# A transformer layer with attention and mixture of experts on one core: second-half gathers that add into x while they are transferred

## The chip, the cores and the metric

The kernel runs on one core of a Trainium2 chip. The metric is the time of one execution on the device, in microseconds (us), lower is better. Three runs of the kernel before gave 713.87, 715.39 and 716.93 us; their median is 715.39 us. A difference of about 0.5% is what a measurement of this kernel can tell from no change.

## The reference

The input is `x` of 32 batches x 256 tokens x 128 features. Each token is normalised, and three things are added up: the input, an attention over the 256 tokens of its batch, and the output of the two best of eight experts for that token.

```python
xn = _layernorm(x)
x = x + attention(xn, Wq, Wk, Wv, Wo, We) + ffn(xn, gate_w, w1, b1, w2, b2)

# attention: 16 heads of 8 features, one more term common to all heads
influence = einsum('bqe,bke->bqk', xn @ We.T, xn @ We.T)
scores = einsum('bhqd,bhkd->bhqk', Q, K) * SCALE + 0.1 * influence[:, None]
out = softmax(scores) @ V ... @ Wo.T

# ffn: the two most probable of 8 experts, weighted by their probabilities
h = gelu(x @ w1[expert] + b1[expert]);  y = h @ w2[expert] + b2[expert]
out = sum over the two choices of y * topk_probs
```

## The kernel before

The 8192 tokens lie as 64 tiles of 128 tokens in `x` (128 partitions, 64 tiles, 128 features, float32), where input and partial results are summed. A batch `b` has the tiles `2b` and `2b+1`. The work has four stages.

**Opening.** Load, normalise, transpose, choose experts for every token. `pos[j]` gets, for each token and each of its two choices `j`, the row of the slot that it occupies in the experts' sorted list.

**Attention for batches 0 to 15 (first half).** One step per batch. A step is a software pipeline over `k`: it projects batch `k+3` (letter `p` in the code), loads the stacked queries and keys of batch `k+2` (`l`), takes plain products and their row maxima for batch `k+1` (`m`), shifted products, exponentials and values for batch `k` (`x`), normalises batch `k-1` (`o`), and adds the attention of batch `k-2` into `x` (`c`, DVE line 970). `attention_steps` writes the first and last steps out and lets a loop on each engine run over the rest, two steps to a turn. A step is 8 units `u`; in each, TensorE makes two shifted products (line 1133), and each raises the semaphore `s_ex` by one, so `s_ex` reaches `16b + n + 1` after the shifted product `n` of batch `b`. ACT takes the exponential of each (line 708) and DVE the maxima of the plain products (line 956). SyncE's queue loads the stack for TensorE (lines 326, 330 and 334, then the maxima at 364 and the projections at 341 to 345), let go by `s_ex`, `s_mt`, `s_hq` and `s_lq`. GpSimd scatters the normalised rows to their slots in DRAM meanwhile (line 565).

**Experts.** 71 tiles of 256 slots go through the experts; the weighted results are stored in `slots_y` in DRAM, one row of 128 floats (512 bytes) per slot.

**Attention for batches 16 to 31 (second half).** The same steps. In addition GpSimd fetches the experts' results. In its loop `n` runs from 0 to 15 (`HALF` is 16) and serves four tiles: the two of batch `n` and the two of batch `16 + n`. Eight indirect DMAs (line 609), `m` from 0 to 7, gather 128 rows each: `j = m // 4` is the choice, `i = m % 4` the tile. They write into the buffer `ye2[n % 2]`, which overlays the tensor `rows`, so the profile calls it `rows`. Each waits until TensorE has reached a place in the step for batch `15 + n` (`LEAD` is 8, so the eight are spread over eight units). `add_choices` (line 594) then adds the second choice's four tiles to the first's, and `add_experts` (line 600) adds the sum into `x`. These two stand in GpSimd's queue behind the gathers `m == 3` and `m == 5` of the next `n`. `s_sum` tells DVE, two steps later, that the experts' part of batch `16 + n` is in `x`; DVE adds the attention's part, raises `s_acc`, and SyncE's queue stores the two batches `n` and `16 + n` (lines 445 and 447).

Nothing but waits and the queues' own order sets the sequence on an engine: each engine runs its own list, written out by the code.

Of the kernel before, what the change touches and what calls it, by code (L numbers as in the profile page):

```python
# [19 lines left out]
F32 = mybir.dt.float32  # L20
# [3 lines left out]
ALU = mybir.AluOpType  # L24
# [4 lines left out]
D = 128  # L29
# [29 lines left out]
LEAD = 8  # L59
HALF = B // 2  # L60
# [72 lines left out]
def build(nc, X, Wsmall, Wo, W12, B1, B2, out):  # L133
    with ExitStack() as ctx:
        def sb(name, shape, dt):
            return ctx.enter_context(nc.sbuf_tensor(name, shape, dt))

        def sem(name):
            return ctx.enter_context(nc.semaphore(name))
# [3 lines left out]
        slots_y = nc.dram_tensor("slots_y", [ET * SLOT, D], F32, kind="Internal").ap()  # L143
# [5 lines left out]
        x = sb("x", [P, NT, D], F32)  # L149
# [32 lines left out]
        pos = [sb(f"pos{i}", [P, NT], U32) for i in range(2)]  # L182
# [32 lines left out]
        free = rows[:, :, :].rearrange("p t d -> p (t d)")  # L215
        at = [0]

        def carve(n, dt):
            v = free[:, at[0]:at[0] + n * (2 if dt == F32 else 1)]
            at[0] += n * (2 if dt == F32 else 1)  # L220
            return v.bitcast(F32) if dt == F32 else v
# [4 lines left out]
        hp = [carve(2 * FC * SLOT, F16).rearrange("p (a f s) -> p a f s", a=2, f=FC) for _ in range(2)]  # L226
        ye = [carve(2 * D, F32).rearrange("p (s d) -> p s d", s=2) for _ in range(4)]
        b2 = carve(NE * D, F32)
        ye2 = [free[:, 16 * D * i:16 * D * (i + 1)].bitcast(F32).rearrange("p (m d) -> p m d", m=8) for i in range(2)]
        assert at[0] <= NT * RW  # L230


# [32 lines left out]
        s_ex, s_xp, s_pv, s_pe = (sem(n) for n in ("s_ex", "s_xp", "s_pv", "s_pe"))  # L265
# [1 line left out]
        s_xr = [sem(f"s_xr{i}") for i in range(4)]  # L267
        s_sp = [sem(f"s_sp{i}") for i in range(3)]
        s_fu, s_fg, s_fh, s_fa, s_fl, s_fd, s_fy = (sem(n) for n in ("s_fu", "s_fg", "s_fh", "s_fa", "s_fl", "s_fd", "s_fy"))
        s_yp, s_both, s_sum = sem("s_yp"), sem("s_both"), sem("s_sum")  # L270
        s_ys = [sem(f"s_ys{i}") for i in range(4)]
        s_yg = [[sem(f"s_yg{r}_{m}") for m in range(8)] for r in range(2)]
        s_cw = [sem(f"s_cw{i}") for i in range(4)]
# [27 lines left out]
        def _(sp):  # L301
            sp.dma_start(ws_stage, Wsmall).then_inc(s_ws, 16)
            for q, sm in enumerate(s_x):
                n = slice(q * NT // 4, (q + 1) * NT // 4)
# [133 lines left out]
            def attend_store(s, f, k):  # L438
                attend(s, f, k, False)
                if f["c"]:  # L440
                    b = s.at(-2)[0]
                    sp.wait_ge(s_acc, b + 1 if isinstance(b, int) else sp.to_reg(b + 1))
                    for n in (b - HALF, b):
                        if isinstance(n, int):
                            sp.dma_start(out_v[n], x[:, 2 * n:2 * n + 2, :]).then_inc(s_out, 16)
                        else:
                            sp.dma_start(out_v[bass.ds(n, 1)].rearrange("n p s d -> (n p) s d"), x[:, bass.ds(2 * n, 2), :]).then_inc(s_out, 16)
# [6 lines left out]
        def _(pool):  # L454
# [56 lines left out]
            for g in range(NG):  # L511
# [5 lines left out]
                for j in range(2):  # L517
                    t = 4 * g + j
# [37 lines left out]
            for j in range(2):  # L556
                for t in range(NT):
                    n = NT * j + t
# [26 lines left out]
            for i, sm in enumerate(s_ys):  # L585
                pool.wait_ge(sm, 16 * ((ET - i + 3) // 4))

            halves = x[:, :, :].rearrange("p (h t) d -> p h t d", h=2)

            def add_choices(n):  # L590

                for m in range(8):
                    pool.wait_ge(s_yg[n % 2][m], 16 * (n // 2) + 16)
                pool.tensor_tensor(ye2[n % 2][:, 0:4, :], ye2[n % 2][:, 0:4, :], ye2[n % 2][:, 4:8, :], ALU.add).then_inc(s_both, 1)

            def add_experts(n):

                pool.wait_ge(s_both, n + 1)
                pair = halves[:, :, 2 * n:2 * n + 2, :]
                pool.tensor_tensor(pair, pair, ye2[n % 2][:, 0:4, :].rearrange("p (h t) d -> p h t d", h=2), ALU.add).then_inc(s_sum, 1)  # L600

            for n in range(HALF):
                for m in range(8):
                    j, i = m // 4, m % 4
                    t = 2 * n + i if i < 2 else 2 * (n + HALF) + i - 2
                    pool.wait_ge(s_ex, 16 * (HALF + n) + 2 * (m - LEAD) + 2)
                    if n >= 2:
                        pool.wait_ge(s_sum, n - 1)
                    pool.indirect_dma_start(ye2[n % 2][:, m, :], None, slots_y, bass.IndirectOffsetOnAxis(pos[j][:, t:t + 1], 0)).then_inc(s_yg[n % 2][m], 16)  # L609
                    if m == 3 and n:  # L610
                        add_choices(n - 1)
                    if m == 5 and n:
                        add_experts(n - 1)
            add_choices(HALF - 1)
            add_experts(HALF - 1)


        @block.scalar
# [144 lines left out]
        def _(dve):  # L763
# [167 lines left out]
            def attend(s, f, k, first_half=True):  # L931
                b, par, half = s.at(0)
                b1_, par1, half1 = s.at(1)
                for u in range(8):
                    if first_half and (k, u) in ((HALF, 2), (HALF, 6), (HALF + 1, 2)):
                        experts.load({(HALF, 2): 3, (HALF, 6): 12}.get((k, u), EW))
                    if first_half and k == HALF and u == 0:
                        dve.wait_ge(s_whi, NCH)
                        for h in range(2):
                            cols = slice((2 * NCH - 2 + h) * WCH // 2, (2 * NCH - 1 + h) * WCH // 2)  # L940
                            dve.scalar_tensor_tensor(out=w12[:, 1, cols], in0=w_stage[:, h * WCH // 2:(h + 1) * WCH // 2], scalar=FS, in1=w12[:, 0, cols], op0=ALU.mult, op1=ALU.subtract).then_inc(s_wlo, 1)
                    if k == -1 and u == 6:
                        prefix()
                    if k == 0 and u == 0:
                        counted()
                    if k == 0 and u == 2:
                        probs()
                    if k == 0 and u == 4:
                        tile_experts()
                    if k == 0 and u == 7:  # L950
                        tile_words()
                    if f["m"]:
                        g, qt = u // 2, u % 2
                        a = g // 2
                        dve.wait_ge(s_mx, 8 * b1_ + u + 1)
                        dve.tensor_reduce(mx[:, a, 8 * qt:8 * qt + 8].rearrange("q (i e w) -> q i e w", i=2, e=2)[:, :, g % 2], MX[u % 2][:, :].rearrange("q (i w k) -> q i w k", i=2, w=2), AX.X, ALU.max).then_inc(s_red, 1)  # L956
                        if u in (3, 7):
                            dve.wait_ge(s_red, 8 * b1_ + 4 * a + 4)
                            if k is None or b1_ >= 2:
                                dve.wait_ge(s_mr[par1][a], 32 * half1)  # L960
                            for i in range(4):
                                ins = dve.transpose(mT[:, par1, a, 32 * i:32 * i + 32], mx[32 * i:32 * i + 32, a, :])  # L962
                            ins.then_inc(s_mt, 1)
                    if u == 0 and f["c"]:
                        bc = s.at(-2)[0]
                        if not first_half:
                            dve.wait_ge(s_sum, bc - HALF + 1)
                        dve.wait_ge(s_wo, bc + 1)
                        xs_ = x[:, 2 * bc:2 * bc + 2, :] if isinstance(bc, int) else x[:, bass.ds(2 * bc, 2), :]
                        dve.tensor_tensor(xs_, xs_, MISC[:, S:2 * S].rearrange("p (q d) -> p q d", q=2), ALU.add).then_inc(s_acc, 1)  # L970
                    if u == 2 and f["p"]:
                        b3_ = s.at(3)[0]
                        dve.wait_ge(s_hq, b3_ + 1)
                        dve.scalar_tensor_tensor(out=lo_qk[:, :, :].rearrange("p a t -> p (a t)"), in0=MISC[:, :], scalar=1 / WS,
                                                 in1=hi_qk[:, :, :].rearrange("p a t -> p (a t)"), op0=ALU.mult, op1=ALU.subtract).then_inc(s_lq, 1)
                    if u == 5 and f["o"]:
                        bo = s.at(-1)[0]
                        dve.wait_ge(s_ot, bo + 1)
                        v = MISC[:, :].rearrange("q (h r) -> q h r", r=16)
                        dve.reciprocal(rden[:, :], v[:, :, DK]).then_inc(s_rd, 1)  # L980
                        dve.wait_ge(s_rd, bo + 1 + c_rd)
                        if k is None or bo >= 1:
                            dve.wait_ge(s_oT, bo)
                        dve.tensor_tensor(o_n[:, :, :, :].rearrange("p q h d -> p (q h) d"), v[:, :, 0:DK], rden[:, :].unsqueeze(2).to_broadcast([P, 2 * H, DK]), ALU.mult).then_inc(s_on, 1)
# [305 lines left out]
```

## Time and profile before

| | |
|---|---|
| runs of the kernel before | 713.87, 715.39, 716.93 us |
| span of the profiled execution | 791.5 us |
| PE, DVE, ACT, POOL busy in it | 671.2, 619.4, 538.9, 467.2 us |
| attention, first half, 116 to 340 us | PE busy 195.61 of 224 us |
| experts, 348 to 536 us | PE busy 187.03 of 188 us |
| entry of the second half, 545 to 570 us | PE busy 12.24 of 25 us |
| second half in its loop, 600 to 745 us | PE busy 131.98 of 145 us |

The profiled execution is one execution and 76.1 us longer than the median of the runs without a profile; what lies around its span is part of that difference and isn't shown apart. Durations below are those of the profiled execution. In the rows, L609 is line 609 of the kernel before, `<-` stands between what is written and what is read, and the brackets at a row's end give how long the engine stood idle before it and which event ended that.

### The profile page before, as it was taken

The page shows a single profiled execution, that of the slowest core. Times are in us where ns is not written, and L with a number is a line of the kernel's source. Part 1 is how long each engine was busy: PE and PEld are TensorE (multiplying, and loading weights), DVE is VectorE, ACT ScalarE, POOL GpSimd, SP SyncE. Part 2 cuts the span into 40 slices and gives each one's busy share as a digit, 9 for nine tenths or more (in the row PEclk, how much of TensorE's full clock was granted, in tenths as well). Part 3 has the DMA queues.
Part 4 walks back from the last instruction along what each step waited for, and adds up shares of the span by engine and source line. Part 5 has one row for each costly group of instructions (what it writes and reads, how often), then busy time and mean ns, then how long its engine had stood idle before and what let it go on. Part 6 is the DMA issues. An engine that isn't in the chain of part 4 may idle for free.

```text
span 791.5 us, 24553 instructions
## 1 busy us (share of the span) xinstructions
PE 671.2 (85%) x7800; PEld 433.1 (55%) x7800; DVE 619.4 (78%) x1106; ACT 538.9 (68%) x1123; POOL 467.2 (59%) x542
## 2 busy tenths in 40 slices
PE   0477888989889896969999999996689989988886
PEld 0463344444444443559999999993244444444444
DVE  8989878878778785948888888885587888887871
ACT  2581566776667685858888888884466766766765
POOL 8650656666566555306555565656676676676671
PEclk9997899999999998999999999999699999999998
DMA  9779545665455653664555454443376666566632
GB/s 262 253 212 299 138 125 146 154 175 158 117 159 148 176 155 100 174 111 90 101 105 102 96 109 102 103 89 100 77 153 161 159 165 166 152 161 161 159 92 61
DMA packets 162947, 113.32 MB, mean 143 GB/s; under 512 B 72624, under 2 KB 150448, under 8 KB 162864
## 3 DMA queue, kind: packets, MB, share of 16 engines
q1 hardware_dynamic: 153632, 90.63, 46.2%
q0 software_dynamic: 8192, 16.86, 8.6%
q10 hardware_dynamic: 1040, 4.76, 1.6%
q8 instruction: 48, 0.79, 0.4%
q14 instruction: 35, 0.29, 0.1%
HBM read 55.42 MB, written 47.19 MB: 130 GB/s over the span
## 4 chain that ended last, share of the span: by engine, by line
PE 71%; DVE 7%; issue 7%; SPq 5%; ACT 4%; another core or an unknown queue 3%; DMA 1%; ACTq 0%; DVEq 0%
PE bank L1133 20%; PE bank L1111 13%; PE bank L1251 12%; PE mx L1240 12%; PE mx L1145 7%; ACT A L708 4%; DVE mx L956 2%; PE bank L1193 2%; PE bank L1031 2%; PE bank L1162 2%; DVE A L791 2%; PE bank L1155 1%; SPq L319 1%; SPq L318 1%
## 5 line engine op out<-in xcount | busy, mean ns | idle before, releaser
L708 ACT ACTIVATE A<-bank 128x512 f32<-128x512 f32 x502 | 279.1, 602 | 109.9 <-PE bank L1133 94.1
L956 DVE TENSOR_REDUCE mx<-mx 128x4 f16<-128x1024 f32 x256 | 303.7, 1208 | 56.3 <-PE mx L1145 26.8
L1133 PE MATMUL bank<-stack 113*128 113x256 f16 x1004 | 185.2, 283 | 51.2 <-issue 24.9
L565 POOL DMA_INDIRECT slots_x<-rows,pos x128 | 123.5, 965 | 91.3 <-PE bank L1133 68.0
L579 POOL TENSOR_SCALAR rows<-rows,slot_p 128x128 f32<-128x128 f32 x142 | 112.1, 798 | 103.4 <-DVE rows L1007 103.4
L609 POOL DMA_INDIRECT rows<-slots_y,pos x128 | 121.5, 950 | 73.4 <-PE bank L1133 54.6
L1133 PEld LDWEIGHTS bank<-stack 113*128 113x128 f16 x1004 | 66.9, 99 | 164.9 <-issue 85.7
L1111 PE MATMUL bank<-A,V 128*32 128x256 f32 x2048 | 142.2, 397 | 1.7 <-ACT A L708 1.6
L752 ACT ACTIVATE rows<-mx,b 128x256 f32<-128x256 f32 x284 | 111.8, 474 | 30.0 <-PE mx L1240 30.0
L1001 DVE TENSOR_TENSOR rows<-rows 128x512 f16<-128x512 f32 x142 | 101.2, 714 | 25.2 <-ACT rows L756 22.8
L1251 PE MATMUL bank<-w,rows 128*128 x1704 | 108.2, 220 | 4.4 <-DVE rows L1001 4.4
L1251 PEld LDWEIGHTS bank<-w,rows 128*128 128x128 f16 x1704 | 102.0, 98 | 6.7 <-issue 4.6
L1240 PE MATMUL mx<-rows,w 128*128 128x256 f16 x852 | 105.4, 274 | 0.0
L1145 PE MATMUL mx<-stack 64*128 64x256 f16 (+1 forms) x1024 | 84.4, 279 | 11.9 <-DVE mx L956 4.5
L1240 PEld LDWEIGHTS mx<-rows,w 128*128 x852 | 80.8, 98 | 8.7 <-issue 0.2
L1111 PEld LDWEIGHTS bank<-A,V 128*32 128x32 f32 x2048 | 54.4, 111 | 50.9 <-issue 23.2
L697 ACT ACTIVATE O<-bank 128x256 f32<-128x256 f32 x64 | 24.7, 386 | 60.0 <-PE bank L1111 34.2
L1145 PEld LDWEIGHTS mx<-stack 64*128 64x128 f16 (+1 forms) x1024 | 36.6, 96 | 52.1 <-issue 30.6
L962 DVE STREAM_TRANSPOSE mT<-mx 32x32 f16<-32x32 f16 x256 | 51.2, 200 | 6.8
L756 ACT ACTIVATE rows<-rows 128x512 f16<-128x512 f32 x71 | 44.8, 630 | 6.7
L970 DVE TENSOR_TENSOR x<-x,bank 128x256 f32 (+1 forms) x32 | 13.5, 421 | 38.1 <-PE bank L1193 25.8
L1052 PE MATMUL mx<-ident,rows 128*128 128x128 f16 x128 | 13.4, 268 | 34.1 <-DVE rows L828 32.5
(142 smaller groups left out, 616.8 us busy)
## 6 DMA issues: line engine op xcount, KB each, us to landing
stack<-ctx_rest SPq DMA_DIRECT2D x64, 256.0 KB
stack<-qk_dram SPq DMA_DIRECT2D x128, 96.0 KB
slots_y<-rows SPq DMA_DIRECT2D x71, 128.0 KB, 2.0
qk_dram<-hi_qk SPq DMA_DIRECT2D x64, 128.0 KB
stack<-ctx_high SPq DMA_DIRECT2D x128, 64.0 KB
slots_x<-A ACTq DMA_DIRECT2D x1, 4644.0 KB, 20.2
w_stage<-in_w SPq DMA_DIRECT2D x8, 512.0 KB
qk_dram<-lo_qk SPq DMA_DIRECT2D x64, 64.0 KB
```

The lines of the kernel that those rows point to most:

```text
L565: pool.indirect_dma_start(slots_x, bass.IndirectOffsetOnAxis(pos[j][:, t:t + 1], 0), rows[:, t, :].bitcast(F32), None).then_inc(s_scat, 16)
L579: ins = pool.tensor_scalar(ye[n % 4][:, h, :], ye[n % 4][:, h, :], slot_p[:, n // 4 % 3, n % 4, h:h + 1], None, ALU.mult)
L609: pool.indirect_dma_start(ye2[n % 2][:, m, :], None, slots_y, bass.IndirectOffsetOnAxis(pos[j][:, t:t + 1], 0)).then_inc(s_yg[n % 2][m], 16)
L708: act.activation(A[:, n % NA, :, :].rearrange("p h s -> p (h s)"), scores(k, n)[:, :], ACT.Exp, scale=SCALE).then_inc(s_xp, 1)
L752: act.activation(h32[r % 2][:, fc, :], bank[fc][:, 0:SLOT], ACT.Gelu_apprx_tanh, bias=b1[:, bass.ds(e + fc, 1)], scale=1 / FS).then_inc(s_ ...
L956: dve.tensor_reduce(mx[:, a, 8 * qt:8 * qt + 8].rearrange("q (i e w) -> q i e w", i=2, e=2)[:, :, g % 2], MX[u % 2][:, :].rearrange("q (i ...
L1001: dve.tensor_tensor(lo, h, hi, ALU.subtract).then_inc(s_fl, 1)
L1111: mm = pe.matmul(PV[32 * i:32 * i + 32, 0:S], head_values(pp, c, g, i), A[:, (4 * g + 2 * c + i // 2) % NA, i % 2, :], start=(e == 0 and c ...
L1133: mm = pe.matmul(scores(k, n)[:, i * S:(i + 1) * S], stack[0:SHIFT + 1, par, h, 1, c * P:(c + 1) * P], stack[0:SHIFT + 1, par, h, 0, :], s ...
L1145: mm = pe.matmul(MX[v % 2][:, (2 * i + p) * S:(2 * i + p + 1) * S], stack[r0:r1, par1, h, 0, v % 2 * P:(v % 2 + 1) * P], stack[r0:r1, par1 ...
L1240: mm = pe.matmul(bank[fc][:, 0:SLOT], w1[:, pa, bass.ds(e + fc * P, P)], xt[r][:, pb, :], start=(n == 0), stop=(n == 2))
L1251: mm = pe.matmul(bank[6 + par][:, h * D:(h + 1) * D], hp[par][:, pa, fc, h * P:(h + 1) * P], w2[:, pb, bass.ds(e_before + fc * P, P)], sta ...
```

## The change

The buffer `ye2` and its two semaphores go. The gather writes with an addition straight into the tile of `x` (`compute_op=ALU.add`): the transfer reads what stands in `x`, adds and writes back. So the two gathers of one tile must not overlap, and the gather of the second choice (`m` 4 to 7) waits for the landing of the first choice's gather of that tile, four gathers before. GpSimd's two additions per `n` go. Each gather's wait on `s_ex` is one lower. DVE, ahead of its addition at batch `16 + n`, waits for the gathers 6 and 7 in the place of `s_sum`, and SyncE's queue, ahead of the stores, for the gathers 4 and 5. All else is the same.

```diff
-        ye2 = [free[:, 16 * D * i:16 * D * (i + 1)].bitcast(F32).rearrange("p (m d) -> p m d", m=8) for i in range(2)]
...
                 if f["c"]:
                     b = s.at(-2)[0]
                     sp.wait_ge(s_acc, b + 1 if isinstance(b, int) else sp.to_reg(b + 1))
+                    for m in (4, 5):
+                        sp.wait_ge(s_yg[s.r][m], 16 * (s.half - 1 - HALF // 2) + 16)
...
-            halves = x[:, :, :].rearrange("p (h t) d -> p h t d", h=2)
-
-            def add_choices(n):
-
-                for m in range(8):
-                    pool.wait_ge(s_yg[n % 2][m], 16 * (n // 2) + 16)
-                pool.tensor_tensor(ye2[n % 2][:, 0:4, :], ye2[n % 2][:, 0:4, :], ye2[n % 2][:, 4:8, :], ALU.add).then_inc(s_both, 1)
-
-            def add_experts(n):
-
-                pool.wait_ge(s_both, n + 1)
-                pair = halves[:, :, 2 * n:2 * n + 2, :]
-                pool.tensor_tensor(pair, pair, ye2[n % 2][:, 0:4, :].rearrange("p (h t) d -> p h t d", h=2), ALU.add).then_inc(s_sum, 1)
-
             for n in range(HALF):
                 for m in range(8):
                     j, i = m // 4, m % 4
                     t = 2 * n + i if i < 2 else 2 * (n + HALF) + i - 2
-                    pool.wait_ge(s_ex, 16 * (HALF + n) + 2 * (m - LEAD) + 2)
-                    if n >= 2:
-                        pool.wait_ge(s_sum, n - 1)
-                    pool.indirect_dma_start(ye2[n % 2][:, m, :], None, slots_y, bass.IndirectOffsetOnAxis(pos[j][:, t:t + 1], 0)).then_inc(s_yg[n % 2][m], 16)
-                    if m == 3 and n:
-                        add_choices(n - 1)
-                    if m == 5 and n:
-                        add_experts(n - 1)
-            add_choices(HALF - 1)
-            add_experts(HALF - 1)
+                    pool.wait_ge(s_ex, 16 * (HALF + n) + 2 * (m - LEAD) + 1)
+                    if j == 1:
+                        pool.wait_ge(s_yg[n % 2][m - 4], 16 * (n // 2) + 16)
+                    pool.indirect_dma_start(x[:, t, :], None, slots_y, bass.IndirectOffsetOnAxis(pos[j][:, t:t + 1], 0), compute_op=ALU.add).then_inc(s_yg[n % 2][m], 16)
...
                         if not first_half:
-                            dve.wait_ge(s_sum, bc - HALF + 1)
+                            for m in (6, 7):
+                                dve.wait_ge(s_yg[s.r][m], 16 * (s.half - 1 - HALF // 2) + 16)
```

GpSimd's list at the start of the second half, before (`rows` is the buffer `ye2`):

```order
262 L609 DMA rows<-slots_y,pos 128x128 [waits s_ys3,s_ys2,s_ex,s_ys1,s_ys0]
263 L609 DMA rows<-slots_y,pos 128x128 [waits s_ex] x11
264 L594 TENSOR_TENSOR rows<-rows 128x512 [waits s_yg0_4,s_yg0_5,s_yg0_3,s_yg0_6,s_yg0_2,s_yg0_7,s_yg0_1,s_yg0_0]
265 L609 DMA rows<-slots_y,pos 128x128 [waits s_ex] x2
266 L600 TENSOR_TENSOR x<-x,rows 128x2x256 [waits s_both]
267 L609 DMA rows<-slots_y,pos 128x128 [waits s_ex] x2
268 L609 DMA rows<-slots_y,pos 128x128 [waits s_sum,s_ex] x4
```

The same place in the changed kernel:

```order
262 L596 DMA x<-slots_y,pos 128x128 [waits s_ys3,s_ys2,s_ex,s_ys1,s_ys0]
263 L596 DMA x<-slots_y,pos 128x128 [waits s_ex] x3
264 L596 DMA x<-slots_y,pos 128x128 [waits s_yg0_0,s_ex]
265 L596 DMA x<-slots_y,pos 128x128 [waits s_yg0_1,s_ex]
266 L596 DMA x<-slots_y,pos 128x128 [waits s_yg0_2,s_ex]
267 L596 DMA x<-slots_y,pos 128x128 [waits s_yg0_3,s_ex]
268 L596 DMA x<-slots_y,pos 128x128 [waits s_ex] x4
269 L596 DMA x<-slots_y,pos 128x128 [waits s_yg1_0,s_ex]
```

Nothing but gathers is left, and the second four of each eight wait for a landing.

DVE's addition of the attention's result, at the steps behind the loop, before:

```order
833 L970 TENSOR_TENSOR x<-x,bank 128x256 [waits s_wo,s_sum]
834 L956 TENSOR_REDUCE mx<-mx 128x2x2 [waits s_mx] x2
835 L974 SCALAR_TENSOR_TENSOR lo_qk<-bank,hi_qk 128x512 [waits s_hq]
836 L956 TENSOR_REDUCE mx<-mx 128x2x2 [waits s_mx]
```

and in the changed kernel:

```order
832 L952 TENSOR_TENSOR x<-x,bank 128x256 [waits s_wo,s_yg0_7,s_yg0_6]
833 L937 TENSOR_REDUCE mx<-mx 128x2x2 [waits s_mx] x2
834 L956 SCALAR_TENSOR_TENSOR lo_qk<-bank,hi_qk 128x512 [waits s_hq]
835 L937 TENSOR_REDUCE mx<-mx 128x2x2 [waits s_mx]
```

It stands in the same place and waits for one semaphore more. The lists of PE and ACT are the same in both kernels.

## Rows read from the trace of the kernel before

**Rows 1.** The page: the span, and busy time of each engine.

```profile
span 791.5 us, 24553 instructions
...
PE 671.2 (85%) x7800; PEld 433.1 (55%) x7800; DVE 619.4 (78%) x1106; ACT 538.9 (68%) x1123; POOL 467.2 (59%) x542
```

**Rows 2.** Busy time by stretch: us, then busy us of each engine.

```profile
core 0: us, PE busy (x) PEld busy (x) DVE busy (x) ACT busy (x) POOL busy (x), PEclk, DMA share, GB/s
...
545.00:570.00 25.00, 12.24 (x98) 4.65 (x92) 7.93 (x11) 8.12 (x16) 17.62 (x18) 0.66 0.42 99
...
600.00:745.00 145.00, 131.98 (x1483) 68.71 (x1476) 124.23 (x199) 101.38 (x207) 100.52 (x99) 1.00 0.66 163
```

**Rows 3.** Waits of PE, 600 to 745 us: engine line, waited for, us, times, longest.

```profile
PE bank L1133 <- ACT A L708: 9.4, 12, 1.1
PE mx L1145 <- issue: 0.8, 4, 0.2
PE mx L1145 <- DVE mx L956: 0.7, 1, 0.7
PE bank L1133 <- issue: 0.7, 2, 0.4
```

**Rows 4.** Timeline of DVE, line 970: start, duration, the instruction, idle before it.

```profile
581.39 0.42 DVE L970 TENSOR_TENSOR x<-x,bank 128x256 f32 x1 [0.92 <-PE bank L1193]
...
743.39 0.42 DVE L970 TENSOR_TENSOR x<-x,bank 128x256 f32<-128x256 f32 x1 [0.85 <-PE bank L1193]
...
788.32 0.42 DVE L970 TENSOR_TENSOR x<-x,bank 128x256 f32<-128x256 f32 x1 [2.30 <-PE bank L1193]
```

**Rows 5.** Groups of instructions of POOL: busy us, mean ns, idle before.

```profile
L609 POOL DMA_INDIRECT rows<-slots_y,pos x128 | 121.5, 950 | 73.4 <-PE bank L1133 54.6 <-issue 13.2 <-remote 3.2
...
L594 POOL TENSOR_TENSOR rows<-rows 128x512 f32<-128x512 f32 x16 | 20.5, 1284 | 3.7 <-DMA rows<-slots_y,pos 3.4
L600 POOL TENSOR_TENSOR x<-x,rows 128x512 f32<-128x512 f32 x16 | 20.4, 1277 | 0.4
```

**Rows 6.** Timeline of POOL: the first gather, part of one step, the last gather.

```profile
542.22 1.05 POOL L609 DMA_INDIRECT rows<-slots_y,pos  x1 [2.73 <-PE bank L1133]
...
618.98 0.95 POOL L609 DMA_INDIRECT rows<-slots_y,pos  x1 [0.16 <-issue]
620.24 0.95 POOL L609 DMA_INDIRECT rows<-slots_y,pos  x1 [0.30 <-issue]
621.21 1.27 POOL L600 TENSOR_TENSOR x<-x,rows 128x512 f32<-128x512 f32 x1
...
625.79 0.94 POOL L609 DMA_INDIRECT rows<-slots_y,pos  x1 [0.89 <-PE bank L1133]
...
772.47 0.95 POOL L609 DMA_INDIRECT rows<-slots_y,pos  x1 [0.30 <-issue]
776.80 1.27 POOL L594 TENSOR_TENSOR rows<-rows 128x512 f32<-128x512 f32 x1 [3.38 <-DMA rows<-slots_y,pos]
```

**Rows 7.** DMA queues and gathers, 600 to 745 us: share of 16 engines.

```profile
q1 hardware_dynamic: 22910, 18.30, 49.4%
q0 software_dynamic: 2538, 5.22, 16.8%
...
rows<-slots_y,pos POOLq DMA_INDIRECT x79
```

**Rows 8.** Timeline of one step: SP's transfer of maxima, the product that needs it.

```profile
618.89 1.36 SPq L364 DMA_DIRECT2D stack<-mT  x2
...
624.15 0.61 PE L1133 MATMUL bank<-stack 113*128 113x256 f16 x4
```

**Rows 9.** Timeline: long idle times of PE, ACT and DVE, first and second half.

```profile
305.87 0.59 PE L1133 MATMUL bank<-stack 113*128 113x256 f16 x2 [4.63 <-issue]
...
551.60 0.38 ACT L697 ACTIVATE O<-bank 128x256 f32<-128x256 f32 x1 [5.21 <-remote]
553.01 0.61 PE L1133 MATMUL bank<-stack 113*128 113x256 f16 x2 [5.63 <-issue]
558.01 1.22 DVE L956 TENSOR_REDUCE mx<-mx 128x4 f16<-128x1024 f32 x1 [11.38 <-remote]
561.51 1.10 PE L1133 MATMUL bank<-stack 113*128 113x256 f16 x4 [3.91 <-issue]
```

More of the change, by code:

```diff
@@ L269, in build @@
         s_fu, s_fg, s_fh, s_fa, s_fl, s_fd, s_fy = (sem(n) for n in ("s_fu", "s_fg", "s_fh", "s_fa", "s_fl", "s_fd", "s_fy"))
-        s_yp, s_both, s_sum = sem("s_yp"), sem("s_both"), sem("s_sum")
+        s_yp = sem("s_yp")
         s_ys = [sem(f"s_ys{i}") for i in range(4)]
```

## The prediction, made before the changed kernel ran

> **What bounds the kernel now.** I read the page's busy times first [rows 1], then the busy times by stretch [rows 2], because only the second half of the attention is touched. In its loop, from 600 to 745 us, PE is busy 131.98 of 145 us, which is 91%; DVE 124.23 us (86%), ACT 101.38 us and POOL 100.52 us (69%). The granted clock is 1.00 there. So the question is what PE waits for, and the view of its waits answers it [rows 3]: ACT for 9.4 us, and DVE and its own issue for 2.2 us. No wait on POOL and none on a DMA stands there. The step takes (743.39 - 581.39) / 11 = 14.73 us by twelve successive additions of DVE [rows 4].
>
> The same view of DVE's line 970 shows where an engine could meet POOL's work, for that instruction holds the wait on `s_sum`: in the 16 steps of the second half the idle before it is ended 14 times by PE's product with `wo`, as in [rows 4], and never by POOL. The reader is to see that POOL's additions have no customer that waits: they are made more than one step before DVE asks.
>
> **The two additions go.** POOL saves 16 x (1.284 + 1.277) = 41.0 us of busy time [rows 5], or 2.56 us per step. All of it lies beside PE's work: POOL holds 8 x 1.26 (one gather starts 1.26 us after the other when nothing holds it [rows 6]) + 2.56 + 0.3 = 12.9 us of the 14.73 us, and then stands until a shifted product lets it go, 0.89 us in the row shown [rows 6]. Worth on the path: 0. After the change POOL needs 10.1 us per step and waits longer for PE.
>
> At the end the last addition starts at 776.80 + 1.3 us and is over by about 779.4, while DVE's last two additions wait for PE, the last starting at 788.32 [rows 4, 6]. Nine microseconds of cover, so the end doesn't move by what leaves POOL: 0.
>
> **The release by the first product, not the second.** It lets a gather start up to one product sooner. The gathers are taken up by nobody for over a step, so 0 again. The clumps (three gathers 1.26 us apart between the additions) turn into single gathers, one per unit, some 14.73 / 8 = 1.84 us apart. That is kinder to the transfers of SP's queue, on which PE doesn't wait now: 0.
>
> **The wait for the first choice's landing.** Behind it in POOL's queue stand only further gathers. A landing takes about 3.38 us from the issue's end, or 776.80 - 772.47 = 4.3 us from its start [rows 6]. The gather waited for is four earlier: 4 x 1.26 = 5.0 us in the burst at the start of the half, 7.4 us in the steady step. So it waits for nothing unless a landing takes 0.7 us longer, and only in the burst; there 12 gathers would be a few us later. Their user, DVE's addition for batch 16, starts at 581.39 [rows 4], 39 us after the first gather. Cost 0, and 0 still if a landing doubles.
>
> **DVE's and SP's waits.** DVE waits for two semaphores where it waited for one, both long raised; it is idle 0.85 to 0.92 us for PE before that instruction [rows 4], which covers the register work of one more wait. Behind it in DVE's queue are the maxima, which PE needs, so without that cover it would cost its own length, bounded by the 0.16 to 0.30 us that POOL's queue shows between two instructions with a wait [rows 6]: 0 to 0.3 us x 16, at most 4.8 us. I take 0. On SP two waits come behind the wait on `s_acc`; the gathers 4 and 5 that they ask for were issued two steps before. Queued behind are the next stack load and stores: 0.
>
> **The gather itself.** No row shows one that adds. Two prices are open. Its instruction on POOL: from 0.95 us as now (lower end: no addition is made on POOL, and nothing excludes a slightly shorter one, which is worth nothing here) up to double, 1.9 us, one more access to name for every row. I take 0.95 to 1.4. POOL falls behind a step only above a pitch of 1.84 us, so above 1.54 us of busy time, and even then starts with two steps in hand: 128 gathers fit between 542.22 and 788.32 less one landing if their pitch is under (788.32 - 3.4 - 542.22) / 128 = 1.90 us [rows 4, 6].
>
> Its time on the DMA engines: queue 0 holds 16.8% of 16 engines in 145 us for 79 gathers, 0.168 x 16 x 145 / 79 = 4.9 engine-us each [rows 7]. Lower end: this, if the addition rides on the copy. Upper end: I take four times, for reading `x`, adding and writing back row by row, where now rows travel together. Queue 1 holds 49.4% [rows 7], so the engines are 66% busy [rows 2] and a step has room for 0.34 x 16 x 14.73 = 80 engine-us, 10 more for each of 8 gathers. They fill up at 14.9 engine-us for a gather, three times today's. The tightest transfer is the row of maxima: SP issues it from 618.89 to 620.25, and PE's product needs it at 624.15 [rows 8], so 3.9 us of which a landing like the gather's, 3.4 us, may be used. By that bound 0.5 us is left; a row of 2 KB should land sooner than a gather of 64 KB, so I take one to two microseconds. Two gathers fall into that time; if each takes 5 engine-us more, that is 10 / 16 = 0.6 us, covered. I take a gather at 1.5 to 2 times today's, and a cost of 0.
>
> Here a rule speaks against the change. The Trainium skill, page "DMA: Bandwidth & Descriptors", section "Rules for kernel authors", says that an accumulating DMA reads its destination and writes it later, with nothing holding the bytes between; so a gather would have three accesses where it has two, 7.4 engine-us by today's price, and be slower to land. Its section "SDMA does more than copy" puts the adders inline in the stream, by which it would stay near 4.9. The sum is 0 by either, and no row here decides between them; it is why the slower rival below gets a fifth.
>
> **The sum.** 0 of 791.5 us in the profiled execution, and so 715.4 us, the median before. The profile is 76.1 us longer than that median, a factor of 0.904. Without a profile the step may be shorter, 14.73 x 0.904 = 13.3 us; that is closer to POOL's 12.9 us, yet POOL's own time would have to stay as it is and its lead of two steps be used up for a gain.
>
> **Rivals.** *The adding gathers crowd the DMA engines* (slower). Place: the transfers at lines 364 and 326 to 334, on which PE's next products wait. It decides from about three times today's price. At 3.3 times the engines would need 0.494 + 3.3 x 0.168 = 1.05 of the step, 0.7 us more for each of some 15 steps, 11 us: 791.5 + 11 = 802, and 725 to 726 us by the factor. At four times it is 1.17, 2.5 us per step, 37 us, 749 us. For it: a read of `x` is added and rows may go singly; the engines are 66% busy. Against it: PE waits for no transfer now. Chance 0.2, at 726 us.
>
> *POOL's gather gets too long* (slower). Over a pitch of 1.90 us DVE's last addition waits: at 2.2 us (1.9 busy + 0.3) it is 0.3 x 128 = 38 us, 750 us. Chance 0.05.
>
> *The entry of the half gets shorter* (faster). At its start, while 14 gathers are issued 1.26 us apart, PE stands 5.63 and 3.91 us, ACT 5.21 us and DVE 11.38 us for something that the profile doesn't name [rows 9]; from 545 to 570 us PE is busy only 12.24 us, at a mean clock of 0.66 [rows 2]. If POOL's gathers or the first additions are behind this, the change could give back up to 5.63 + 3.91 = 9.5 us, 8.6 us by the factor: 707 us. Against it: the burst of the first twelve gathers stays, and PE stood just so for 4.63 us at 305.87 [rows 9], in the first half. Chance 0.18.
>
> *The change doesn't show because the additions were hidden* is my forecast: same, 715.4 us, chance 0.55, its own range 712 to 719. The last 0.02 is for slower by waits of DVE that lose their cover, up to 4.8 us: 720.
>
> **How the numbers follow.** Faster than 711.8 us: 0.18. Within 0.5%, which is about what a measurement of this kernel can tell from no change: 0.55. Slower than 719.0 us: 0.2 + 0.05 + 0.02 = 0.27. The range of 8 in 10 holds the forecast, most of the faster case and the lower half of the crowding: 707 to 728 us. Outside are the crowding above 3.4 times (about 0.08), POOL's (0.05) and the ends of the faster case (0.06).
>
> **What would show it.** Right: the step between DVE's additions stays within 0.1 us of 14.73; PE's waits name ACT and not a DMA; POOL's busy time falls by 41 us; POOL waits for PE's products before nearly every gather. DMA engines crowded: queue 0 above 50% of the engines in the loop, waits of PE on `stack`. POOL's instruction grown: a mean above 1.54 us, no idle before it. The faster rival: PE's idle between 545 and 570 us halved. I would be wrong if an idle time that the profile doesn't name hung on POOL's additions, or if without a profile POOL were the last.

## The result and the profile after

The changed kernel takes 746.57 us in the median of four runs (742.63 to 747.38), against 716.16 us for the kernel before on the same chips. The ratio is 1.042, with a 95% interval of 1.038 to 1.045: **slower by 4.2%, 30 us**. The forecast was no change.

Its page, to be held against [rows 1]: POOL's busy time rose by 36.5 us, though 41 us of additions are gone.

```profile
span 745.6 us, 24430 instructions
...
PE 653.8 (88%) x7800; PEld 434.4 (58%) x7800; DVE 616.0 (83%) x1106; ACT 542.5 (73%) x1123; POOL 503.7 (68%) x510
```

The span, 745.6 us, is close to the time of the runs, where the profiled execution of before had 791.5 us for 715.4. That execution of before was drawn out in both halves of the attention, which the first experiment shows; what follows compares with the kernel before profiled again.

The costliest group of POOL, where [rows 5] had 950 ns (columns: busy us, mean ns, idle before it):

```profile
L596 POOL DMA_INDIRECT x<-slots_y,pos x128 | 198.2, 1548 | 41.5 <-issue 22.0 <-PE bank L1115 14.0 <-DMA x<-slots_y,pos 4.6
```

A gather that adds takes 1.55 us of GpSimd where a plain one takes 0.95. 128 of them cost 76.6 us more, nearly twice what the additions were worth. The names behind `<-` are not long waits: every gap between two gathers of this kernel is 0.30 to 0.32 us, whatever it is put down to. The waits of DVE, 520 to 746 us (us in total, times, longest), and of PE:

```profile
DVE x L952 <- DMA x<-slots_y,pos: 39.7, 10, 12.3
```

```profile
PE bank L1013 <- DVE x L952: 10.0, 6, 2.9
PE bank L1144 <- DVE x L952: 6.0, 1, 6.0
PE mx L1127 <- DVE mx L937: 2.4, 1, 2.4
...
PE mx L1127 <- DMA stack<-qk_dram: 0.8, 1, 0.8
```

Where [rows 3] named ACT, PE now waits for DVE's addition into `x` (line 952), and DVE for the last gather of its batch. PE's wait on a transfer of SP is 0.8 us in all.

How the wait builds up can be read in the timeline of DVE's line 952, the step's clock of [rows 4] (start, duration, idle before it):

```profile
525.53 0.42 DVE L952 TENSOR_TENSOR x<-x,bank 128x256 f32 x1
538.73 0.42 DVE L952 TENSOR_TENSOR x<-x,bank 128x256 f32 x1
551.95 0.42 DVE L952 TENSOR_TENSOR x<-x,bank 128x256 f32 x1
565.15 0.42 DVE L952 TENSOR_TENSOR x<-x,bank 128x256 f32 x1
581.73 0.42 DVE L952 TENSOR_TENSOR x<-x,bank 128x256 f32 x1 [3.39 <-DMA x<-slots_y,pos]
```

and in POOL's, the first gather and the last five:

```profile
503.67 1.65 POOL L596 DMA_INDIRECT x<-slots_y,pos  x1 [2.73 <-PE bank L1115]
...
731.63 1.55 POOL L596 DMA_INDIRECT x<-slots_y,pos  x1 [0.30 <-DMA x<-slots_y,pos]
733.49 1.55 POOL L596 DMA_INDIRECT x<-slots_y,pos  x1 [0.30 <-DMA x<-slots_y,pos]
735.34 1.55 POOL L596 DMA_INDIRECT x<-slots_y,pos  x1 [0.30 <-issue]
737.19 1.55 POOL L596 DMA_INDIRECT x<-slots_y,pos  x1 [0.30 <-issue]
739.04 1.55 POOL L596 DMA_INDIRECT x<-slots_y,pos  x1 [0.30 <-issue]
```

The reader is to see two rates. DVE's first steps are 13.2 us apart. POOL starts a gather every 1.85 us, 14.8 us for eight. The eight for batch 16 are issued by 503.67 + 14.8 = 518.5 us; DVE asks at 525.53. Each further batch costs 1.6 us of that lead. Batch 20 is issued by 503.67 + 5 x 14.8 = 577.7 us and due at 565.15 + 13.2 = 578.4, less than a landing later: there DVE waits for the first time. The last gather of batch 20 has left GpSimd at 577.55 us and DVE is let go at 581.73, 4.2 us later; behind the last gather of all it is 1.8 us. From batch 20 on the step is POOL's.

At the end the last gather's issue is over at 740.59. DVE adds at 742.42 us, after 12.32 us of idleness, and the span ends 3 us later:

```profile
742.42 0.42 DVE L952 TENSOR_TENSOR x<-x,bank 128x256 f32<-128x256 f32 x1 [12.32 <-DMA x<-slots_y,pos]
```

So the time is 503.67 us to the first gather, 236.9 us of gathers, 1.8 us of landing and 3.2 us of addition and store: 745.6 us.

### The profile page after: what moved, and what is told of

It reads as the page before. It is cut to its first block, busy times and chain, and to the rows that moved or that the text cites. A ratio compares the mean times of both kernels' runs of the same rounds, so it can differ in the third digit from the quotient of the medians.

```text
span 745.6 us, 24430 instructions
## 1 busy us (share of the span) xinstructions
PE 653.8 (88%) x7800; PEld 434.4 (58%) x7800; DVE 616.0 (83%) x1106; ACT 542.5 (73%) x1123; POOL 503.7 (68%) x510
## 3 DMA queue, kind: packets, MB, share of 16 engines
q0 software_dynamic: 22528, 16.86, 13.5%
## 4 chain that ended last, share of the span: by engine, by line
PE 62%; DVE 11%; DMA 11%; SPq 4%; issue 4%; POOL 4%; ACT 2%; POOLq 0%; DVEq 0%; ACTq 0%
PE bank L1233 13%; PE mx L1222 12%; PE bank L1115 12%; PE bank L1093 11%; PE mx L1127 6%; DMA x<-slots_y,pos 6%; DVE mx L937 4%; POOL x L596 4%; DMA stack<-qk_dram 3%; PE bank L1013 3%; DVE A L772 2%; PE bank L1137 1%; PE bank L1175 1%; PE bank L1144 1%; DMA x<-in_x 1%
## 5 line engine op out<-in xcount | busy, mean ns | idle before, releaser
L596 POOL DMA_INDIRECT x<-slots_y,pos x128 | 198.2, 1548 | 41.5 <-issue 22.0
L580 POOL TENSOR_SCALAR rows<-rows,slot_p 128x128 f32<-128x128 f32 x142 | 112.0, 798 | 99.8 <-DVE rows L989 99.8
L1115 PE MATMUL bank<-stack 113*128 113x256 f16 x1004 | 171.9, 278 | 1.4 <-ACT A L689 0.6
L1093 PE MATMUL bank<-A,V 128*32 128x256 f32 x2048 | 138.8, 389 | 1.7 <-ACT A L689 1.7
L1115 PEld LDWEIGHTS bank<-stack 113*128 113x128 f16 x1004 | 72.8, 98 | 90.7 <-ACT A L689 54.4
L1127 PE MATMUL mx<-stack 64*128 64x256 f16 (+1 forms) x1024 | 87.4, 278 | 14.9 <-DVE mx L937 8.5
L1127 PEld LDWEIGHTS mx<-stack 64*128 64x128 f16 (+1 forms) x1024 | 33.6, 95 | 60.8 <-DVE mx L937 25.9
L952 DVE TENSOR_TENSOR x<-x,bank 128x256 f32 (+1 forms) x32 | 13.5, 421 | 43.4 <-DMA x<-slots_y,pos 39.7
L1034 PE MATMUL mx<-ident,rows 128*128 128x128 f16 x128 | 13.7, 272 | 35.5 <-DVE rows L809 33.8
```

The lines of the kernel that those rows point to most:

```text
L580: ins = pool.tensor_scalar(ye[n % 4][:, h, :], ye[n % 4][:, h, :], slot_p[:, n // 4 % 3, n % 4, h:h + 1], None, ALU.mult)
L596: pool.indirect_dma_start(x[:, t, :], None, slots_y, bass.IndirectOffsetOnAxis(pos[j][:, t:t + 1], 0), compute_op=ALU.add).then_inc(s_yg[n ...
L1093: mm = pe.matmul(PV[32 * i:32 * i + 32, 0:S], head_values(pp, c, g, i), A[:, (4 * g + 2 * c + i // 2) % NA, i % 2, :], start=(e == 0 and c ...
L1115: mm = pe.matmul(scores(k, n)[:, i * S:(i + 1) * S], stack[0:SHIFT + 1, par, h, 1, c * P:(c + 1) * P], stack[0:SHIFT + 1, par, h, 0, :], s ...
L1127: mm = pe.matmul(MX[v % 2][:, (2 * i + p) * S:(2 * i + p + 1) * S], stack[r0:r1, par1, h, 0, v % 2 * P:(v % 2 + 1) * P], stack[r0:r1, par1 ...
```

## The experiments

Three theories stood. A: GpSimd's instruction got longer, and its queue of 128 gathers sets the second half. B: the adding transfers load the DMA engines, and transfers land late. C: the new waits (for a landing, on DVE and SP) or the earlier release cost the time. Each experiment's ratio is to runs of the kernel before on the same chip.

### The kernel before, profiled again

> The kernel before, unchanged, profiled once more. In the changed kernel's trace a step of the first half (the same code in both) takes 13.4 us, in the shown profile of before 15.5 us. If that execution was drawn out as a whole, this one has a span near 715 us, a step of 13.2 to 13.4 us in both halves, and GpSimd's 12.9 us of work per step stays as it was, so that it is the fullest but one. If the change itself had made the first half shorter, this span is near 790 us again.

Measured: 715.21 us in its one run, span 713.5 us. The timeline of DVE's line 970, first and second half:

```profile
165.20 0.42 DVE L970 TENSOR_TENSOR x<-x,bank 128x256 f32 x1
178.76 0.42 DVE L970 TENSOR_TENSOR x<-x,bank 128x256 f32 x1
...
578.60 0.42 DVE L970 TENSOR_TENSOR x<-x,bank 128x256 f32 x1
591.81 0.42 DVE L970 TENSOR_TENSOR x<-x,bank 128x256 f32 x1
...
710.25 0.42 DVE L970 TENSOR_TENSOR x<-x,bank 128x256 f32<-128x256 f32 x1 [1.78 <-PE bank L1193]
```

Busy times from 520 to 660 us (us, then PE, PEld, DVE, ACT, POOL, granted clock, DMA share, GB/s), to be held against [rows 2]:

```profile
520.00:660.00 140.00, 139.76 (x1589) 76.19 (x1587) 131.14 (x213) 111.39 (x223) 115.46 (x114) 1.00 0.77 182
```

The step is 13.2 us, not 14.73; PE is busy for 99.8% of it, not 91%. GpSimd's two groups kept their length:

```profile
L609 POOL DMA_INDIRECT rows<-slots_y,pos x128 | 121.6, 950 | 37.1 <-issue 19.0 <-PE bank L1133 14.2 <-POOL x L600 2.1
...
L594 POOL TENSOR_TENSOR rows<-rows 128x512 f32<-128x512 f32 x16 | 20.6, 1286 | 2.2 <-DMA rows<-slots_y,pos 2.0
```

So in the shown execution the step was stretched and the instructions were not. In the first half a step takes 13.5 us here, a little over the expected 13.4. How much of a step GpSimd needs can be read from its timeline, at the first addition of two successive `n`:

```profile
568.00 1.29 POOL L594 TENSOR_TENSOR rows<-rows 128x512 f32<-128x512 f32 x1
...
580.35 1.29 POOL L594 TENSOR_TENSOR rows<-rows 128x512 f32<-128x512 f32 x1
```

Eight gathers and two additions take 12.35 us, and no gap between them is longer than 0.31 us: GpSimd works at its own pace, 0.9 us per step faster than PE. The 12.9 us of the prediction and of the expectation were 0.5 too many.

### Plain gathers into x

```diff
-pool.indirect_dma_start(x[:, t, :], None, slots_y, ..., compute_op=ALU.add).then_inc(...)
+pool.indirect_dma_start(x[:, t, :], None, slots_y, ...).then_inc(...)
```

> The changed kernel with its gathers writing plainly into x, no addition in the transfer: what it leaves out is the addition of the experts' results (x is overwritten by them). Waits, order and releases are those of the changed kernel. Theory A (GpSimd's instruction got longer) and theory B (the adding transfers load the DMA engines) both expect about 716 us, A with a gather of 0.95 us and 10.1 us of GpSimd per step. Theory C (the waits for landings, the release by the first product, or the waits of DVE and SP cost the time) expects 746 us.

Measured: 715.20 us, ratio to before 1.001 (0.999 to 1.003). All of the new waits and the new release are in it, and it loses nothing: theory C is out. (Nor do the waits show on GpSimd in the changed kernel: its gaps are 0.30 to 0.32 us before gathers with one wait and with two.) It gains nothing either, though GpSimd has 10.1 us per step and stands idle for PE:

```profile
L596 POOL DMA_INDIRECT x<-slots_y,pos x128 | 122.2, 955 | 73.1 <-PE bank L1115 63.8 <-issue 7.6 <-DMA x<-slots_y,pos 1.7
```

That confirms the prediction's term for the two additions by a run: without them, and at the old price of a gather, nothing is gained.

### Plain gathers, GpSimd kept as busy as by adding ones

```diff
+filler = free[:, 0:2 * 740].bitcast(F32)
...
-pool.indirect_dma_start(x[:, t, :], ..., compute_op=ALU.add).then_inc(...)
+pool.indirect_dma_start(x[:, t, :], ...).then_inc(...)
+if 8 * n + m:
+    pool.wait_ge(s_filler, 8 * n + m)
+pool.memset(filler, 0.0).then_inc(s_filler, 1)
```

> As e2 (plain gathers into x, so the experts' addition is left out), and behind each gather GpSimd clears 740 words of a scratch area, about 0.7 us, so that it starts a gather every 1.85 to 1.95 us as the changed kernel does, with the DMA engines loaded as in e2. Theory A: 128 starts at that pitch set the second half, 746 us or, at 1.95 us, up to 760. Theory B: 716 us.

Measured: 746.38 us, ratio 1.046 (1.043 to 1.049), the changed kernel's time within 0.2 us, with a span of 745.2. Its groups:

```profile
L597 POOL DMA_INDIRECT x<-slots_y,pos x128 | 123.2, 962 | 24.3 <-issue 16.0 <-PE bank L1119 8.2 <-PE mx L1119 0.2
...
L600 POOL MEMSET rows<- 128x740 f32 x128 | 93.7, 732 | 0.1
```

DVE waits as in the changed kernel, 35.5 us in 8 waits:

```profile
DVE x L956 <- DMA x<-slots_y,pos: 35.5, 8, 12.4
```

No transfer adds here, and the DMA share from 520 to 660 us is 0.66. GpSimd's time alone gives the whole loss: eight gathers with their filling take 14.9 us here, against 14.8 in the changed kernel. The wait that names a DMA is a wait for a gather that GpSimd issued late.

### Four of eight gathers add

```diff
-compute_op=ALU.add
+**({"compute_op": ALU.add} if j == 1 else {})
```

> The changed kernel, but only the second choice's four gathers of each eight add; the first choice's four write plainly, so x loses the input there (left out). GpSimd needs 4 x 1.25 + 4 x 1.85 = 12.4 us per step, under the step's 13.2. Theory A: no cost, 716 to 718 us. Theory B: about half of the loss, 731 us.

Measured: 713.10 us, ratio 1.000 (0.998 to 1.002). Theory B is out as well: the DMA engines are busier than in the changed kernel, 0.81 against 0.79, and nothing is lost. First this kernel, then the changed one, 520 to 660 us:

```profile
520.00:660.00 140.00, 138.84 (x1585) 76.18 (x1588) 130.64 (x210) 110.92 (x222) 112.08 (x89) 1.00 0.81 179
```

```profile
520.00:660.00 140.00, 131.69 (x1476) 70.06 (x1473) 121.91 (x196) 103.62 (x206) 116.80 (x77) 0.99 0.79 163
```

POOL's is the last number before the clock: 112.08 us busy with 89 instructions here, 116.80 with 77 there; the DMA share stands behind the clock.

### Six of eight gathers add

```diff
-compute_op=ALU.add
+**({"compute_op": ALU.add} if m >= 2 else {})
```

> As e4, but six of each eight gathers add (m from 2 to 7) and two write plainly, so x loses the input in the first half's tiles (left out). If GpSimd's queue alone sets the second half, its 128 starts take 16 x (2 x 1.255 + 6 x 1.85) = 217.8 us from 503.7 us on, and 5 us and the 1.5 us around the span follow: 728 us. A cost in proportion to the number of adding gathers would give 714 + 0.75 x 30 = 737 us.

Measured: 729.03 us, ratio 1.023 (1.020 to 1.026). The sum by GpSimd's queue was 728, a cost in proportion 737. With none, four, six and eight adding gathers the times are 715.2, 713.1, 729.0 and 746.6 us: flat, then steep. In the timelines the eight gathers take 12.5 us with four that add, 13.7 with six and 14.8 with eight. What they may take is not the step's 13.2 us but 12.7, eight times the limit of 1.59 us worked out in the next section, for GpSimd's first gather is issued with the half already running and DVE's last additions come sooner than a step after each other. Six are 1.0 us over it, 16 us in 16 steps, and 15.6 were measured. With six, DVE waits for a gather first at 684.54 us, in its 13th step, where the changed kernel did in its fifth. That is what an engine looks like that goes from covered to last.

### The second choice adds onto the buffer, one addition kept

```diff
-            def add_choices(n): ...
             def add_experts(n):
-                pool.wait_ge(s_both, n + 1)
+                for m in range(4, 8):
+                    pool.wait_ge(s_yg[n % 2][m], 16 * (n // 2) + 16)
...
-pool.indirect_dma_start(ye2[n % 2][:, m, :], None, slots_y, ...)
+if j == 1:
+    pool.wait_ge(s_yg[n % 2][m - 4], 16 * (n // 2) + 16)
+pool.indirect_dma_start(ye2[n % 2][:, i, :], None, slots_y, ..., **({"compute_op": ALU.add} if j else {}))
```

> A complete kernel between the two: the first choice's four gathers write plainly into the buffer, the second choice's add onto them there, and GpSimd adds the buffer to x as before; one of its two additions per step goes. GpSimd needs 4 x 1.255 + 4 x 1.85 + 1.43 = 13.85 us per step, more than the 12.9 of before and than the step's 13.2. GpSimd's queue as the bound: 503.7 + 221.6 + 3.4 for the last landing + 1.3 for the last addition + about 4: 732 to 736 us. If the two additions on GpSimd were what mattered, it would be at or under before's 715.

Measured: 727.72 us, ratio 1.021 (1.018 to 1.023): slower, by the mechanism expected, but 4 us under the range. The timeline of its POOL shows three terms that were too large:

```profile
501.45 1.04 POOL L606 DMA_INDIRECT rows<-slots_y,pos  x1 [2.73 <-PE bank L1127]
...
600.84 1.28 POOL L595 TENSOR_TENSOR x<-x,rows 128x512 f32<-128x512 f32 x1
...
614.49 1.29 POOL L595 TENSOR_TENSOR x<-x,rows 128x512 f32<-128x512 f32 x1
...
717.17 1.53 POOL L606 DMA_INDIRECT rows<-slots_y,pos  x1 [0.30 <-issue]
720.58 1.26 POOL L595 TENSOR_TENSOR x<-x,rows 128x512 f32<-128x512 f32 x1 [1.88 <-DMA rows<-slots_y,pos]
```

Its first gather starts at 501.45, not at 503.7, and the last landing takes 1.88 us after the issue, not 3.4. The largest term is the queue: from the first gather's start to the last one's end it is 217.3 us, not 221.6. The last addition had been counted twice, and a step takes 13.65 us, not 13.85, since an addition stands in the place of a gap of 0.30 us: it costs the queue 1.28 + 0.16 - 0.30 = 1.1 us, not 1.43. One addition saved doesn't pay for four gathers at 0.6 us more.

### The changed kernel with the old release

```diff
-pool.wait_ge(s_ex, 16 * (HALF + n) + 2 * (m - LEAD) + 1)
+pool.wait_ge(s_ex, 16 * (HALF + n) + 2 * (m - LEAD) + 2)
```

> The changed kernel with the gathers released by a unit's second shifted product, as before. GpSimd's queue as the bound: no difference to the changed kernel, 746 us, since the queue is behind its releases. If the earlier release helps or hurts, some us either way.

Measured: 745.76 us (745.02 to 746.43), ratio to before 1.046 (1.043 to 1.049), against 746.57 us and 1.042 for the changed kernel in its own runs: no gain or loss that these can tell apart from the chips' differences. The first gather starts 1.5 us sooner than in the changed kernel and the last 1.6, so the queue is as full:

```profile
502.16 1.65 POOL L596 DMA_INDIRECT x<-slots_y,pos  x1 [2.73 <-PE bank L1115]
...
737.41 1.55 POOL L596 DMA_INDIRECT x<-slots_y,pos  x1 [0.30 <-issue]
```

### What the instruction costs

```diff
-pool.indirect_dma_start(x[:, t, :], ..., compute_op=ALU.add)
+# m 0 to 3 add, m 4 to 7 are plain; each: 128 rows of 512 B, 128 of 256 B, 64 of 512 B, 32 of 512 B
+pool.indirect_dma_start(x[0:rows_, t, 0:cols_], ...)
```

> To measure the gather's instruction: the changed kernel with eight forms for m from 0 to 7: adding with 128 rows of 512 bytes, 128 rows of 256 bytes, 64 rows of 512, 32 rows of 512; then plain with the same four. What the other gathers would bring is left out. If the cost of adding is one per row, the adding gathers take 1.55, 1.55, some 1.25 and 1.1 us; if it is a fixed entry, 1.55 in all four; if it goes by bytes, the second is near 1.25.

Measured: one run, 714.27 us. The timeline of POOL for one `n`; the order of the rows is that of `m`:

```profile
575.96 1.58 POOL L597 DMA_INDIRECT x<-slots_y,pos  x1 [0.30 <-issue]
577.84 1.57 POOL L597 DMA_INDIRECT x<-slots_y,pos  x1 [0.31 <-issue]
579.71 1.42 POOL L597 DMA_INDIRECT x<-slots_y,pos  x1 [0.30 <-issue]
581.44 1.34 POOL L597 DMA_INDIRECT x<-slots_y,pos  x1 [0.30 <-DMA x<-slots_y,pos]
583.09 1.00 POOL L597 DMA_INDIRECT x<-slots_y,pos  x1 [0.30 <-DMA x<-slots_y,pos]
584.40 0.96 POOL L597 DMA_INDIRECT x<-slots_y,pos  x1 [0.30 <-DMA x<-slots_y,pos]
585.67 0.93 POOL L597 DMA_INDIRECT x<-slots_y,pos  x1 [0.30 <-issue]
586.90 0.88 POOL L597 DMA_INDIRECT x<-slots_y,pos  x1 [0.30 <-PE bank L1116]
```

None of the three readings fits fully. The order has a part in these rows: in the run with four adding gathers, where all have 128 rows of 512 bytes, the four plain ones take 1.00, 0.98, 0.94 and 0.94 us and the four adding ones 1.58, 1.56, 1.54 and 1.54. Held against the gather in the same place there, halving the bytes changes nothing (1.57 against 1.56, 0.96 against 0.98). A quarter of the rows saves 0.20 us in adding and 0.06 plainly, so a row costs some 2 and 0.6 ns. At 32 rows adding still costs 1.34 against 0.88: most of the surcharge, 0.46 of 0.60 us, is there at 32 rows too. A smaller adding gather therefore isn't the way out. Together the eight need 12.1 us with their gaps, and the kernel runs at before's pace.

No version beat the kernel before. PE is busy 139.76 of 140 us in the loop there, and the plain gathers, which relieve GpSimd most, gained nothing.

## Why the prediction was wrong

**What bounds the kernel.** PE, rightly, but by the wrong margins. I read the step as 14.73 us from an execution whose span exceeded the runs by 76 us. The step is 13.2 us. POOL's own need was misread as well, the other way: 12.9 us counts each addition on top of a 0.30 us gap whose place it takes. The second profile shows 12.35 us, so the room was 0.9 us, half of the 1.8 that I had counted on. (Between the two additions of an `n` stand two gathers and between those of successive `n` six, not three.)

**The additions: 0.** Right, shown by the plain gathers, 715.2 us.

**The release and the waits for landings: 0.** Right, by the same run and by the old release, 745.8 us. In the run with plain gathers POOL waits for PE 63.8 us, as I expected of the changed kernel. There it never gets to that: its queue is always behind.

**The gather's instruction and its cover: the step that failed.** I put the longer instruction on POOL at a cost of 0. Its price was bounded by 0.95 and 1.9 us and taken as "0.95 to 1.4". It is 1.55, inside the bounds, above my value and just above the 1.54 that I had named as the point where POOL falls behind a step; the sign that I gave for it, a mean above 1.54 us and no idle before it, is what the trace shows. But the right price alone would still have given 0, for its pitch of 1.85 us is under my limit of 1.90. The limit is what failed most. It was worked out from the stretched execution. With the first gather of the kernel before at 503.72 us in its second profile, and its last addition at 710.25, it is (710.25 - 3.4 - 503.72) / 128 = 1.59 us; the pitch is 1.85, and even the 1.4 us that I allowed would have made 1.7. The prediction divided its final sum by the factor between profile and runs, yet held GpSimd's fixed time against undivided steps. With the factor on the stretch alone the same formula gives 1.90 x 0.904 = 1.72 us, below the 1.85 that an instruction of 1.55 makes, and the rival with a chance of 0.05 decides well inside my own bounds for its price. (The factor was too mild for this stretch: from the first gather to DVE's last addition the two profiles have 246.1 and 206.5 us, a factor of 0.84.) My last line, that I would be wrong if POOL were the last without a profile, named the case: before the change it was not, with the longer gathers it was.

**"Starts with two steps in hand".** Wrong as well. DVE's first addition follows 525.53 - 503.67 = 21.9 us after the first gather, of which the first eight gathers take 14.8. The lead was 7 us less a landing, and it was gone after four batches.

**The gather on the DMA engines.** The size was right, 1.5 to 2 times, and so was its cost of 0. Queue 0, changed kernel, 520 to 660 us, held against [rows 7]:

```profile
q0 software_dynamic: 10891, 4.96, 30.0%
...
x<-slots_y,pos POOLq DMA_INDIRECT x77
```

That is 0.30 x 16 x 140 / 77 = 8.7 engine-us for each, 1.8 times the 4.9 of before; I had taken 1.5 to 2. The Trainium skill, "DMA: Bandwidth & Descriptors", section "Rules for kernel authors", says that an accumulating DMA reads its destination and writes it later. The higher time agrees with the added read, though no run shows the read by itself. Neither of the two readings that I weighed, 4.9 and 7.4, reaches 8.7. The rival of crowded DMA engines, to which I gave a fifth, falls: PE waits 0.8 us for a transfer of SP, and four adding gathers, with a DMA share of 0.81, cost nothing.

**The entry of the half.** The idle times of [rows 9] belonged to that one execution. In the second profile of before, PE is busy 24.49 of the 25 us from 505 to 530 us, and DVE's first addition follows the first gather by 21.9 us (525.61 - 503.72), where the shown one needed 39 us.

**The rival that came true** had the right place and mechanism: POOL's gathers too long, DVE's last addition waiting. Its price was worked out at 0.3 us x 128 over a limit that was 0.3 us too high; with the measured pitch and limit it is (1.85 - 1.59) x 128 = 33 us, and 32.2 us were measured between the last additions of DVE (742.42 and 710.25).

## What to carry to other kernels

Before you trade a covered engine's arithmetic for a feature of its transfers, price the issuing instruction: here a gather that adds cost its issuing engine 0.6 us more, eight times per step, to save two additions that took 2.3 us of its queue. Hold a fixed duration only against a step taken from an execution whose span matches the runs; where the profile is 10% longer than the runs, take the slack of every covered engine by the shorter step, or you give it room that it doesn't have. A wait that names a DMA can be a wait for its issuer; look at the issuing queue's idle time first.

## What the runs showed of the hardware

- An indirect gather of 128 rows takes GpSimd 0.95 us plain and 1.55 us with an addition; of 32 rows 0.88 and 1.34 us. The bytes per row made no difference between 256 and 512. Between two such instructions lie 0.30 us, also where the second's waits were long fulfilled; a GpSimd addition in between takes the place of one of these gaps and adds 1.1 us to the queue.
- In the same 140 us, 77 adding gathers made 10891 packets on queue 0, 141 each, and took 8.7 engine-us each. In the run with plain gathers 93 made 2958, 32 each:

```profile
q0 software_dynamic: 2958, 6.06, 20.3%
```

- That is 0.203 x 16 x 140 / 93 = 4.9 engine-us for a plain one. So the plain gather's 128 rows travel at least four to a packet, and the adding one's about one to a packet.
- One profiled execution of the same kernel can be 11% longer than another (791.5 and 713.5 us) with DVE's and GpSimd's instructions at the same length: the difference lay mostly in idle time (PE was busy 671.2 and 651.5 us), in the first half of the attention as well as in the second (11 steps of the first half from 116.28 to 290.06 us, 15.8 us each, against 13 from 111.16 to 286.38, 13.5 us each). What caused it stays open; no run here looked for it.
